# Learning loop with one gradient product per weight matrix, an early sum for weights 20, a new order of the loop's instructions, and expert tables made in two parts

## The chip, the cores and the metric

The kernel runs on one core of a Trainium2 chip. A core has TensorE (PE in the rows; its weight loads are PEld), VectorE (DVE), ScalarE (ACT), GpSimd (POOL) and SyncE (SP), each with a queue of its own that is worked off in order, and 16 DMA engines. The metric is the device time of one execution in microseconds (us), as the median over several runs. Everything is float32 unless a row says bf16.

## The reference

The input x is (4, 32, 32, 128). Three layers with residual sums follow each other: a memory that learns while it reads (the part that takes most of the time), a banded additive attention, and a top-2 mixture of 8 experts.

```python
def step(carry, x_t):                     # 32 steps, one after the other
    params, mom = carry                   # per batch b: w1_0, w2_0, w1_1, w2_1
    k = _l2norm(x_t @ Wk); v = x_t @ Wv   # 32 tokens of 128 per batch and step
    lr, forget, eta = ...                 # one number per batch and step
    g = grad_fn(params, k, v)             # of mean((mlp(params, k) - v) ** 2)
    new_mom = eta * mom - lr * g
    new_params = params * (1.0 - forget) + new_mom
...                                       # _mlp: h = h + gelu(h @ w1) @ w2, two layers
xn = (xt - mu) * rsqrt(var + LN_EPS)      # experts: 4096 tokens
probs = softmax(xt @ Wr + br); top_p, top_idx = top_k(probs, 2)
h = gelu(xe @ W1 + b1); y = h @ W2 + b2   # the two chosen of 8 experts, weighted and summed
```

## The kernel before, in words

The program is a row of blocks written out by hand: `prepare` (norms and projections), `learn` (the 32 steps), `read_out`, the attention, `experts`. In each block every engine has its own list of instructions, and semaphores alone tie the lists together. The order in a list is the order in the code. No scheduler moves anything.

**The learning loop (`learn`).** All four batches are worked on at once: a tile of 128 partitions holds 4 batches of 32 tokens. The four weight matrices are called 10 and 20 (first layer, up and down) and 11 and 21 (second layer). For each there are `W` (weights, 128 x 4 x 256, in the rows `s_w`), `M` (momentum, `s_w_mem`) and `KW` (weights times 1 - forget, `s_xsh`). The loop is rotated: one turn runs `backward(t)` and then `forward(t)`, which finishes step t and starts step t+1. Thirty-one turns follow each other, and `last` closes the block. Along a turn runs one chain, in which TensorE, ScalarE and VectorE take turns. Its VectorE instructions have names by which the turn can be cut in pieces:

- `l_h` (h1, the output of layer 1), then `l_g<-lp_b` on ScalarE (gelu of layer 2, called gelu1 below),
- `l_dp` (the error, dp), after it `l_dd`, `l_v` and `l_gp` (the slope of gelu in three instructions: `weighted`, `bent`, `slope`),
- `l_da<-l_gp,lp_a` (da1), `l_dh` (dh1), `l_da<-l_gp,lp_b` (da0), and so to the next `l_h`.

Between two of these lie a transpose on TensorE (`turn`), a copy out of PSUM on ScalarE (`feature`) and a product on TensorE (`up` or `down`, four batches side by side in strips of 32).

Beside the chain lies the upkeep of the weights. TensorE makes the gradient of a matrix in four PSUM banks `lp_g`, one per batch (`grad_1`, `grad_2`). VectorE then makes the new momentum of each batch (`momentum`, 16 instructions a turn). ScalarE or GpSimd makes KW (`keep_of`), and GpSimd (`add`, for 21, 11 and 10) or VectorE (`update`, for 20) makes W = KW + M. All four gradients go through the same banks, so a gradient waits until the momentum of the one before is done. Before the change a turn has six gradient groups: 20 and 11 are split into two pairs of batches each (`D11A, D11B, D20A, D20B`), 21 and 10 are whole (`D21, D10`). (The number names the momentum that the group feeds.) TensorE also transposes W of 21, 11 and 20 (`turn_w`, two halves each), and ScalarE copies them out (`wt`).

**The expert block (`experts`).** The 4096 tokens are routed in four groups (`routed(g)`, g = 0 to 3). GpSimd scatters every group's rows to their expert's region in DRAM (`f_xg`, 16 scatters a group). When all groups are routed, VectorE works out tables for 39 jobs of 256 rows: which expert owns a job (`owner_i`, `mine`) and at which row it starts (`start_i`). Jobs 0 to 16 (`NA` = 17) read only rows of the first three groups. SP loads a job's rows (`f_xt`), TensorE turns them (`turn(j)`) and multiplies, and 39 jobs follow each other at an even pace. SP starts with

```python
sp.wait_ge(owner_ready, 4)
sp.wait_ge(sent, 16 * 2 * GT * (GR - 1))      # scatters of groups 0 to 2
```

and TensorE, before its first job, makes the bias table from `mine` and runs 20 matmuls whose result is not used (`unused`).

Of the kernel before, what the change touches and what calls it, by code (L numbers as in the profile page):

```python
# [305 lines left out]
def learn(nc, st, sb):  # L306

    sem = lambda name: st.enter_context(nc.semaphore(name))
    with ExitStack() as ctx:
# [20 lines left out]
        ps_g = [bank(f"g{b}") for b in range(B)]  # L330
# [14 lines left out]
        G21, G11, G20, G10 = range(4)  # L345
        D21, D11A, D11B, D20A, D20B, D10 = range(1, 7)
# [32 lines left out]
        with nc.Block() as block:  # L379
# [10 lines left out]
            def _(pool):  # L390
# [21 lines left out]
                def forward(p, grads=True):  # L412
                    t = p + 1
                    if grads:
                        for k in ("21", "20", "10"):
                            pool.wait_ge(kept[k], p * 2 + 2)
                        pool.wait_ge(kept["11"], p * 2 + 2)
                    nc.gpsimd.tensor_copy(keep_lr[:, :], step_of(t, "coef")[:, 4:9]).then_inc(lr_in, 1)  # L418
                    pool.wait_ge(lr_in, t + 1)
                    nc.gpsimd.tensor_tensor(keep[:, :], keep_lr[:, 0:B], none[:, :], ALU.subtract).then_inc(keep_in, 1)  # L420
                    if grads:
                        add(p, "21", G21, 1)
                    if grads:
                        pool.wait_ge(grad_done, p * 6 + D10)
                    nc.gpsimd.tensor_copy(kc[:, :], step_of(t, "ktok")).then_inc(kc_ready, 1)
                    if grads:
                        add(p, "11", G11, 1)
                    keep_of(t, "11", 0)
                    if grads:
                        add(p, "10", G10, 0)  # L430
                    nc.gpsimd.tensor_copy(kx[:, :], step_of(t + 1, "kf")).then_inc(kx_ready, 1)
                    if grads:
                        pool.wait_ge(mom_ready, mom(p, G10, 1))
                    nc.gpsimd.tensor_copy(eta[:, :], step_of(t, "coef")[:, 0:4]).then_inc(eta_in, 1)
# [4 lines left out]
                    scaled(kk, keep).then_inc(kk_ready, 1)
                    keep_of(t, "11", 1)  # L440
                    if grads:
                        add(p, "10", G10, 1)

                def backward(t):
                    add(t, "21", G21, 0)
                    pool.wait_ge(mm_done, t * 7 + A0)
# [1544 lines left out]
```

## Time and profile before

| | before |
|---|---|
| three runs | 956.37, 959.83, 960.83 us, median 959.83 us |
| the profiled execution | 957.53 us, its span 955.7 us |
| busy share of the span | PE 85%, DVE 76%, ACT 65%, POOL 64% |
| one turn of the loop | 15.24 us, 31 turns |
| granted clock in the loop | 1.00 of 2.4 GHz |

The span is the time from the first to the last instruction of the profiled execution. A turn's length is the distance of two starts of the same instruction in neighbouring turns. The shares are averages over blocks with different limits, so what the change is worth is read within the loop and within the start of the expert jobs.

### The profile page before, as it was taken

Reading aid. Unit: us, or ns where it says so; the run is one execution under the profiler, and the core shown is the slowest. Engines: PE = TensorE matmul, PEld = TensorE weight load, DVE = VectorE, ACT = ScalarE, POOL = GpSimd, SP = SyncE. Lnnn points to the kernel's source line nnn. Section 1 sums busy time; section 2 is a strip of 40 time slices with the busy share of each in tenths; the row PEclk is TensorE's granted clock in tenths of the full one; section 3 lists DMA queues with packets and bytes.
Section 4 is the critical chain, followed back from the end, with each engine's and each line's share of the span. In section 5 each row is a group of like instructions: output and inputs, shape, how many; then the busy total and the mean of one; then the engine's idle time right before and its main releaser. Section 6 shows DMA issues by size and latency. Waiting matters only on the chain. (4 is left out here: it accounts for less than half of the span.)

```text
span 955.7 us, 25199 instructions
## 1 busy us (share of the span) xinstructions
PE 809.4 (85%) x8049; PEld 506.4 (53%) x8049; DVE 726.0 (76%) x1861; ACT 618.9 (65%) x1384; POOL 608.6 (64%) x758
## 2 busy tenths in 40 slices
PE   2788999999999999999999989965678777999950
PEld 2455555555555555555555544431246544999940
DVE  3586888888888888888888871578798875777747
ACT  4577777778777787877777753228823523888830
POOL 1127888878788887878788739940004777666650
PEclk8899999999999999999999999987998978999985
DMA  7006999996000000000000005005000113233327
GB/s 239 1 2 140 159 208 158 81 6 2 0 0 0 0 0 0 0 0 0 0 0 0 0 5 157 18 11 185 1 4 29 52 51 90 82 93 93 92 68 239
DMA packets 105406, 54.10 MB, mean 57 GB/s; under 512 B 42624, under 2 KB 96664, under 8 KB 105360
## 3 DMA queue, kind: packets, MB, share of 16 engines
q1 hardware_dynamic: 98976, 43.34, 28.9%
q0 software_dynamic: 4544, 9.38, 3.0%
q10 hardware_dynamic: 1840, 0.79, 0.3%
q8 instruction: 26, 0.43, 0.2%
q14 instruction: 20, 0.16, 0.1%
HBM read 21.49 MB, written 29.44 MB: 53 GB/s over the span
## 5 line engine op out<-in xcount | busy, mean ns | idle before, releaser
L398 POOL TENSOR_TENSOR s_w<-s_xsh,s_w_mem 128x512 f32<-128x512 f32 x186 | 252.0, 1355 | 9.0 <-DVE s_w_mem L570 3.5
L570 DVE SCALAR_TENSOR_TENSOR s_w_mem<-s_w_mem,s_eta,lp_g 128x256 f32<-128x256 f32 x496 | 218.0, 476 | 23.9 <-PE lp_g L733 18.6
L495 ACT ACTIVATE s_xsh<-s_w,l_keep_lr 128x256 f32<-128x256 f32 x384 | 173.9, 507 | 17.5 <-POOL l_keep_lr L418 17.5
L1489 POOL DMA_INDIRECT f_yg<-f_yr,f_xmeta x78 | 78.3, 1004 | 38.4 <-DVE f_yr L1857 25.6
L1484 POOL DMA_INDIRECT f_xg<-f_xrow,f_place x64 | 64.0, 1000 | 49.3 <-DVE f_place L1750 30.4
L403 POOL TENSOR_TENSOR s_xsh<-s_w,l_keep 128x512 f32<-128x512 f32 x64 | 72.0, 1125 | 0.0
L1464 ACT ACTIVATE f_hh<-fp_v,f_bcol 128x256 f32<-128x256 f32 x156 | 61.4, 476 | 14.4 <-DVE f_hs_lo L1848 8.5
L489 ACT COPY l_wt<-lp_b 128x512 f32<-128x512 f32 x96 | 56.5, 588 | 15.0 <-PE lp_b L719 15.0
L719 PE MATMUL lp_b<-s_cst,s_w 128*128 128x128 f32 x384 | 61.7, 284 | 0.0
L1594 PE MATMUL fp_v<-f_xf,s_w_hi 128*128 128x256 bf16 x312 | 54.4, 276 | 3.3 <-DVE f_xmeta L1837 2.7
L707 PE MATMUL lp_h<-s_w,l_gf 128*32 128x128 f32 x1024 | 41.4, 278 | 18.3 <-ACT l_gf L482 18.3
L719 PEld LDWEIGHTS lp_b<-s_cst,s_w 128*128 128x128 f32 x384 | 43.0, 141 | 23.2 <-DVE l_gp L602 13.2
L1848 DVE TENSOR_TENSOR f_hs_lo<-f_hh,f_hs_hi 128x512 bf16<-128x512 f32 x52 | 33.6, 688 | 21.4 <-ACT f_hs_hi L1470 21.4
L579 DVE TENSOR_TENSOR s_w<-s_xsh,s_w_mem 128x512 f32<-128x512 f32 x62 | 48.0, 775 | 1.1
L733 PE MATMUL lp_g<-l_dh,l_g 32*128 32x128 f32 x496 | 44.2, 296 | 0.0
L1177 DVE TENSOR_TENSOR t_h<-s_qp,s_kp 128x1056 f32<-128x1056 f32 x32 | 37.6, 1255 | 8.5 <-ACT s_kp L1200 8.3
L707 PEld LDWEIGHTS lp_h<-s_w,l_gf 128*32 128x32 f32 x1024 | 25.0, 109 | 35.4 <-issue 25.1
L726 PE MATMUL lp_g<-l_da,l_h 32*128 32x256 f32 x248 | 43.4, 426 | 0.0
L1594 PE MATMUL fp_v<-f_xf,s_w_lo 128*128 128x256 bf16 x156 | 43.1, 276 | 0.0
L489 ACT COPY l_wt<-lp_a 128x512 f32<-128x512 f32 x64 | 37.7, 589 | 6.7 <-PE lp_a L719 6.7
L719 PE MATMUL lp_a<-s_cst,s_w 128*128 128x128 f32 x256 | 42.0, 286 | 0.0
L733 PEld LDWEIGHTS lp_g<-l_dh,l_g 32*128 32x128 f32 x496 | 32.4, 185 | 16.5 <-DVE s_w_mem L570 12.8
(360 smaller groups left out, 2040.7 us busy)
## 6 DMA issues: line engine op xcount, KB each, us to landing
f_xg<-s_pad SPq DMA_DIRECT2D x1, 17280.0 KB, 108.2
f_xt<-f_xg SPq DMA_DIRECT2D x39, 130.0 KB
r_w<-in_L_ffn_W_dram SPq DMA_DIRECT2D x16, 256.0 KB, 3.2
s_w<-f_yg SPq DMA_DIRECT2D x16, 256.0 KB, 3.8
xs<-in_x_dram SPq DMA_DIRECT2D x4, 512.0 KB, 7.0
t_w<-in_L_ffn_W_dram SPq DMA_DIRECT2D x8, 256.0 KB
out_dram<-s_x SPq DMA_DIRECT2D x8, 256.0 KB, 3.1
s_xsh<-s_xl SPq DMA_DIRECT2D x4, 448.0 KB, 3.5
```

What stands on the lines that cost most here:

```text
L398: nc.gpsimd.tensor_tensor(W[k][:, half(h), :], KW[k][:, half(h), :], M[k][:, half(h), :], ALU.add).then_inc(w_ready[k], 1)
L403: nc.gpsimd.tensor_tensor(KW[k][:, half(h), :], W[k][:, half(h), :], keep[:, half(h)].rearrange("p (b a) -> p b a", a=1).to_broadcast([128 ...
L489: nc.scalar.copy(flat(WT[k][:, half(h), :]), wt_bank(k, h)).then_inc(wt_ready, 1)
L495: m = nc.scalar.mul(KW[k][:, b, :], W[k][:, b, :], keep_lr[:, b:b + 1])
L570: i = nc.vector.scalar_tensor_tensor(out=M[k][:, b, :], in0=M[k][:, b, :], scalar=eta[:, b:b + 1], in1=ps_g[b][:, 0:256], op0=ALU.mult, op ...
L707: i = nc.tensor.matmul(p[rows(b), 0:128], x[:, 128 * h + 32 * b:128 * h + 32 * b + 32], w[:, b, 128 * h:128 * h + 128], start=h == 0, stop ...
L719: i = nc.tensor.transpose(wt_bank(k, h)[:, 128 * j:128 * j + 128], W[k][:, 2 * h + j // 2, 128 * (j % 2):128 * (j % 2) + 128], ident)
L733: i = nc.tensor.matmul(ps_g[b][:, 128 * h:128 * h + 128], x[rows(b), 128 * h:128 * h + 128], y[rows(b), :], start=True, stop=True)
L1464: nc.scalar.activation(hh[j % 2][:, h, :], ps_h[j % 2][:, SL * h:SL * h + SL], ACT.Gelu, bias=bcol[:, h, j:j + 1]).then_inc(h_ready, 1)
L1484: nc.gpsimd.indirect_dma_start(sb["xg"][:, :], bass.IndirectOffsetOnAxis(ap=place[:, g, k, i:i + 1], axis=0), row[k][:, tile_of(g, i), :], ...
L1489: nc.gpsimd.indirect_dma_start(sb["yg"][:, :], bass.IndirectOffsetOnAxis(ap=xmeta[:, j, a, 0:1].bitcast(mybir.dt.int32), axis=0), yr[j % R ...
L1594: m = nc.tensor.matmul(p, chosen(w1s[b], e, h), xf[j % 2][:, c, :], start=r == 0, stop=r == 2)
```

## The change

Five things change in the loop, one in the expert block.

1. Each gradient is made for four batches in one group (`D21, D11, D20, D10`): two groups a turn less on TensorE.
2. Weights 20: instead of `momentum` and then W = KW + M in two halves, VectorE first makes P = eta * M + KW for each batch (`decayed_20`, four new instructions, before the gradient is there), then W = P + gradient for all four batches in one instruction of 1024 elements that reads PSUM (`update_20`). The momentum of 20 is still made, after it.
3. The momenta are made in another order of batches, each with a semaphore step of its own, and at other places of VectorE's list.
4. On TensorE the gradient of 21 stands ahead of the transpose of dp, the gradient of 10 behind the transpose of h1, and `turn_w("20", 1)` behind the product for gelu1. ScalarE copies that one out after gelu1 (`wt(t, X20B, ...)` moved from `forward` to `backward`) and makes the KW pieces in another order.
5. GpSimd copies `kx` at the head of its `forward`, makes `ke` in `backward`, and makes the adds of 11 in a row.
6. The tables of jobs 0 to 16 are worked out between the third and the fourth group's routing (`first_tables`). The rest follows after the fourth. SP waits for the first part only, and for the second at job 17.

```diff
-        ps_g = [bank(f"g{b}") for b in range(B)]
+        ps_all = bank("g", B)
+        ps_g = [ps_all[:, 512 * b:512 * b + 512] for b in range(B)]
...
-        D21, D11A, D11B, D20A, D20B, D10 = range(1, 7)
+        D21, D11, D20, D10 = range(1, 5)
+        KEEPS = {"21": (0, 2, 3, 1), "20": (0, 1, 2, 3), "10": (2, 0, 1, 3), "11": (0, 1, 2, 3)}
...
+                def decayed_20(t, b):
+
+                    dve.wait_ge(eta_in, t + 1)
+                    dve.wait_ge(kept["20"], kept_of(t, "20", (b,)))
+                    dve.wait_ge(mom_ready, mom(t - 1, "20", (b,)))
+                    nc.vector.scalar_tensor_tensor(out=P[:, b, :], in0=M["20"][:, b, :], scalar=eta[:, b:b + 1],
+                                                   in1=KW["20"][:, b, :], op0=ALU.mult, op1=ALU.add).then_inc(decayed_ready, 1)
+
+                def update_20(t):
+
+                    dve.wait_ge(decayed_ready, 4 * t + 4)
+                    dve.wait_ge(grad_done, t * 4 + D20)
+                    nc.vector.tensor_tensor(W["20"][:, :, :], P[:, :, :],
+                                            ps_all[:, :].rearrange("p (b n) -> p b n", b=B)[:, :, 0:256], ALU.add).then_inc(w_ready["20"], 4)
...
-                    momentum(t, "21", D21, (0,))
+                    momentum(t, "21", D21, 2, 3, 0)
                     slope_times(t, 1, ps_a, DG1)
-                    momentum(t, "21", D21, (1,))
-                    momentum(t, "21", D21, (2, 3))
-                    momentum(t, "11", D11A, (0, 1))
+                    momentum(t, "21", D21, 1)
+                    decayed_20(t, 0)
+                    decayed_20(t, 2)
+                    momentum(t, "11", D11, 0)
                     dve.wait_ge(mm_done, t * 7 + DH1)
...
-                sp.wait_ge(owner_ready, 4)
+                sp.wait_ge(owner_ready, 3)
                 sp.wait_ge(sent, 16 * 2 * GT * (GR - 1))
                 for j in range(NJ):
                     if j == NA:
+                        sp.wait_ge(owner_ready, 6)
                         sp.wait_ge(sent_last, 16 * 2 * GT)
...
+                def first_tables():
+                    filled(carry_a[:, :], tiles_a)
...
+                    beyond(0, NA, ends_a[:, 1:E])
+                    owners(0, NA)
...
+                    gaps(0, NA, gap_a)
+                    dve.wait_ge(owner_ready, 2)
+                    link(nc.vector.tensor_reduce(owner[:, 0:NA], past[:, 0:NA, :], AX.X, ALU.add))
+                    nc.vector.tensor_tensor(start_i[:, 0:NA], owner[:, 0:NA], job[:, 0:NA], ALU.add).then_inc(owner_ready, 1)
+
                 def routed(g):
                     bias_piece(2 * g)
+                    if g == GR - 1:
+                        first_tables()
                     dve.wait_ge(lg_done, 2 * g + 2)
```

**Where VectorE's list changes first: from the slope to da1.** Before, in `backward` (`s_w_mem` is a momentum, `l_da` da1; REGISTER_ALU and ISA rows prepare waits):

```order
L602 SCALAR_TENSOR_TENSOR l_gp<-l_v,lp_b 128x256
L567 REGISTER_ALU
L570 SCALAR_TENSOR_TENSOR s_w_mem<-s_w_mem,s_eta,lp_g 128x256
L607 REGISTER_ALU
L608 SCALAR_TENSOR_TENSOR l_da<-l_gp,lp_a 128x256
L570 SCALAR_TENSOR_TENSOR s_w_mem<-s_w_mem,s_eta,lp_g 128x256 x5
```

The same place now (`l_p` is the new early sum for weights 20):

```order
L626 SCALAR_TENSOR_TENSOR l_gp<-l_v,lp_b 128x256
L583 ISA
L586 REGISTER_ALU
L587 SCALAR_TENSOR_TENSOR s_w_mem<-s_w_mem,s_eta,lp_g 128x256 x2
L586 REGISTER_ALU
L587 SCALAR_TENSOR_TENSOR s_w_mem<-s_w_mem,s_eta,lp_g 128x256
L631 REGISTER_ALU
L632 SCALAR_TENSOR_TENSOR l_da<-l_gp,lp_a 128x256
L587 SCALAR_TENSOR_TENSOR s_w_mem<-s_w_mem,s_eta,lp_g 128x256
L594 ISA
L595 SCALAR_TENSOR_TENSOR l_p<-s_w_mem,s_eta,s_xsh 128x256
```

Three momenta stand ahead of da1 instead of one. Behind it come one momentum, two early sums and one more momentum instead of five momenta.

**The second place on VectorE: from da0 to h1.** Before (the two `s_w` rows are the two halves of `update`):

```order
L608 SCALAR_TENSOR_TENSOR l_da<-l_gp,lp_b 128x256
L578 ISA
L579 TENSOR_TENSOR s_w<-s_xsh,s_w_mem 128x512
L567 REGISTER_ALU
L570 SCALAR_TENSOR_TENSOR s_w_mem<-s_w_mem,s_eta,lp_g 128x256 x2
L578 REGISTER_ALU
L579 TENSOR_TENSOR s_w<-s_xsh,s_w_mem 128x512
L583 ISA
L584 SCALAR_TENSOR_TENSOR l_u<-l_q,lp_a 128x256
L590 SCALAR_TENSOR_TENSOR l_dd<-l_q,l_g 128x256
```

And now:

```order
L632 SCALAR_TENSOR_TENSOR l_da<-l_gp,lp_b 128x256
L594 REGISTER_ALU
L595 SCALAR_TENSOR_TENSOR l_p<-s_w_mem,s_eta,s_xsh 128x256
L587 SCALAR_TENSOR_TENSOR s_w_mem<-s_w_mem,s_eta,lp_g 128x256
L602 TENSOR_TENSOR s_w<-l_p,lp_g 128x1024
L587 SCALAR_TENSOR_TENSOR s_w_mem<-s_w_mem,s_eta,lp_g 128x256 x2
L637 ISA
L638 ISA
L638 TENSOR_TENSOR l_h<-lp_h,s_ktok 128x128
L587 SCALAR_TENSOR_TENSOR s_w_mem<-s_w_mem,s_eta,lp_g 128x256
```

The two updates became one with 1024 elements, and `l_u` and `l_dd` of the next step moved behind `l_h`.

**The place in the expert block, VectorE ahead of the fourth group's router.** Now (`f_tilesa`, `f_endsa`, `f_past`, `f_owner`: tables of the first 17 jobs; `f_lg` is the first instruction of the fourth group's routing):

```order
L1763 TENSOR_TENSOR f_tilesa<-f_endsa 128x8
L1747 TENSOR_TENSOR f_past<-s_job,f_endsa 128x119
L1751 TENSOR_REDUCE f_owner<-f_past 128x17
L1752 CAST f_owneri<-f_owner 128x17
L1753 TENSOR_SCALAR f_mine<-f_owner,s_cst 128x17
L1766 TENSOR_SCALAR f_gapa<-f_tilesa 128x7
L1756 TENSOR_TENSOR f_past<-f_past,f_gapa 128x119
L1769 TENSOR_REDUCE f_owner<-f_past 128x17
L1770 TENSOR_TENSOR f_starti<-f_owner,s_job 128x17
L1779 TENSOR_TENSOR f_lg<-fp_y,f_s 128x64
```

Before, all of it stood behind the fourth group, and `f_owner` and `f_past` were made for 39 jobs at once. Fourteen instructions moved ahead, and sixteen are left behind the fourth group where 26 stood.

## Rows read from the trace of the kernel before

**Rows 1.** The page: its first line, and the costliest group of copies on ScalarE (count | busy us, mean ns)

```profile
span 955.7 us, 25199 instructions
...
L489 ACT COPY l_wt<-lp_b 128x512 f32<-128x512 f32 x96 | 56.5, 588 | 15.0 <-PE lp_b L719 15.0
```

**Rows 2.** Busy time per engine in one turn (us, instructions, granted clock)

```profile
302.42:317.66 15.24, 14.58 (x175) 8.53 (x171) 12.86 (x33) 11.79 (x30) 12.51 (x17) 1.00 0.00 0
```

**Rows 3.** Instructions in order of time, VectorE, one turn (start us, duration us)

```profile
302.42 0.42 DVE L608 SCALAR_TENSOR_TENSOR l_da<-l_gp,lp_b 128x256 f32<-128x256 f32 x1
...
302.75 0.69 DVE L579 TENSOR_TENSOR s_w<-s_xsh,s_w_mem 128x512 f32<-128x512 f32 x1
...
304.25 0.87 DVE L579 TENSOR_TENSOR s_w<-s_xsh,s_w_mem 128x512 f32<-128x512 f32 x1
...
306.17 0.29 DVE L620 TENSOR_TENSOR l_h<-lp_h,s_ktok 128x128 f32<-128x128 f32 x1 [0.38 <-PE lp_h L707]
...
310.43 0.35 DVE L637 SCALAR_TENSOR_TENSOR l_dp<-lp_h,l_keep_lr,l_hv 128x128 f32<-128x128 f32 x1 [0.72 <-PE lp_h L707]
...
310.70 0.57 DVE L590 SCALAR_TENSOR_TENSOR l_dd<-l_q,l_g 128x256 f32<-128x256 f32 x1
...
312.57 0.42 DVE L608 SCALAR_TENSOR_TENSOR l_da<-l_gp,lp_a 128x256 f32<-128x256 f32 x1
...
312.90 2.21 DVE L570 SCALAR_TENSOR_TENSOR s_w_mem<-s_w_mem,s_eta,lp_g 128x256 f32<-128x256 f32 x5
...
315.02 0.28 DVE L648 TENSOR_TENSOR l_dh<-lp_h,l_dp 128x128 f32<-128x128 f32 x1
...
317.66 0.42 DVE L608 SCALAR_TENSOR_TENSOR l_da<-l_gp,lp_b 128x256 f32<-128x256 f32 x1
```

**Rows 4.** The same turn, TensorE and ScalarE

```profile
303.16 0.70 PE L745 MATMUL lp_a<-l_da,l_sk 128*128 128x256 f32 x2
...
308.21 0.38 ACT L468 ACTIVATE l_g<-lp_b 128x256 f32<-128x256 f32 x1
...
308.49 0.38 ACT L471 ACTIVATE l_q<-lp_b 128x256 f32<-128x256 f32 x1
...
311.10 0.73 PE L733 MATMUL lp_g<-l_dp,l_g 32*128 32x128 f32 x16
...
315.85 0.33 PE L713 MATMUL lp_t<-s_cst,l_dh 128*128 128x128 f32 x1
...
316.11 0.71 PE L733 MATMUL lp_g<-l_dh,l_g 32*128 32x128 f32 x8
```

**Rows 5.** The same turn, GpSimd

```profile
302.39 0.19 POOL L418 COPY l_keep_lr<-s_coef 128x5 f32 x1 [1.15 <-ACT s_xsh L495]
...
302.81 1.76 POOL L398 TENSOR_TENSOR s_w<-s_xsh,s_w_mem 128x512 f32<-128x512 f32 x1
...
305.90 1.28 POOL L398 TENSOR_TENSOR s_w<-s_xsh,s_w_mem 128x512 f32<-128x512 f32 x1
...
307.14 1.04 POOL L403 TENSOR_TENSOR s_xsh<-s_w,l_keep 128x512 f32<-128x512 f32 x1
```

**Rows 6.** Instructions in order of time, VectorE, the loop's last step

```profile
556.76 1.28 DVE L658 SCALAR_TENSOR_TENSOR s_w_mem<-s_w_mem,s_eta,s_xsh 128x256 f32<-128x256 f32 x2
```

**Rows 7.** Instructions in order of time, start of the expert jobs

```profile
779.80 0.23 DVE L1719 TENSOR_TENSOR f_lg<-fp_y,f_s 128x64 f32<-128x64 f32 x1 [3.05 <-PE fp_y L1532]
...
787.84 0.29 DVE L1794 TENSOR_TENSOR f_over<-f_carrya,s_lim 128x128 f32<-128x128 f32 x1
...
792.34 5.09 PE L1118 MATMUL fp_y<-s_w_hi 128*128 128x384 bf16 x20
...
795.48 18.55 SPq L1394 DMA_DIRECT2D f_xt<-f_xg  x8
...
799.30 0.40 PE L1565 MATMUL fp_x<-f_identb,f_xt 128*128 128x128 bf16 x4 [0.91 <-DMA f_xt<-f_xg]
```

**Rows 8.** Waits of SP's queue (waits for what: us in total, times, longest)

```profile
SPq L1393 <- DVE f_bcol L1829: 3.1, 1, 3.1
```

More of the change, by code:

```diff
@@ L360, in step_of, with mom, kept_of, weights_of @@
             return sb[k][:, bass.ds(t, 1), :].rearrange("p a n -> p (a n)")
-        def mom(t, n, h):
-            return t * 8 + 8 + 2 * n + h + 1
+        def mom(t, k, batches=range(B)):
+            return t * 16 + 16 + max(MOMENTA.index((k, b)) for b in batches) + 1
+        def kept_of(t, k, batches):
+            return t * 4 + max(KEEPS[k].index(b) for b in batches) + 1
+        def weights_of(t, k, h):
+            return t * 4 + 2 * HALVES[k].index(h) + 2
+        def of_half(h):
+            return (2 * h, 2 * h + 1)
         def wt_bank(k, h):
@@ L420, in forward @@
-                    nc.gpsimd.tensor_tensor(keep[:, :], keep_lr[:, 0:B], none[:, :], ALU.subtract).then_inc(keep_in, 1)
                     if grads:
[L422 to L427, printed above, removed]
+                        add(p, "11", 0)
@@ L428, in forward @@
                     keep_of(t, "11", 0)
                     if grads:
[L430 to L434, printed above, removed]
+                        add(p, "11", 1)
+                        pool.wait_ge(grad_done, p * 4 + D10)
@@ L435, in forward @@
+                    nc.gpsimd.tensor_copy(kc[:, :], step_of(t, "ktok")).then_inc(kc_ready, 1)
+                    keep_of(t, "11", 1)
                     pool.wait_ge(mm_done, t * 7 + A0)
                     pool.wait_ge(kx_ready, t + 1)
+                    pool.wait_ge(keep_in, t + 1)
+                    scaled(kk, keep).then_inc(kk_ready, 1)
+                    if grads:
+                        add(p, "10", 0)
+                        pool.wait_ge(mom_ready, mom(p, "10"))
+                    nc.gpsimd.tensor_copy(eta[:, :], step_of(t, "coef")[:, 0:4]).then_inc(eta_in, 1)
@@ L437, in forward, with backward @@
+                    if grads:
+                        add(p, "10", 1)
+                def backward(t):
+                    add(t, "21", 1)
+                    keep_for(t + 1)
                     pool.wait_ge(eta_in, t + 1)
                     scaled(ke, eta).then_inc(ke_ready, 1)
[L439 to L446, printed above, removed]
+                    add(t, "21", 0)
@@ L763, in forward @@
                     turn(h1, 128)
-                    pe.wait_ge(chain, t * 6 + K_HV)
-                    turn_w("20", 1)
-                    pe.wait_ge(w_ready["11"], t * 2 + 2)
+                    if grads:
+                        pe.wait_ge(mom_ready, mom(p, "20"))
+                        pe.wait_ge(kc_ready, p + 1)
+                        grad_1(kc, da[0], range(B))
+                    pe.wait_ge(w_ready["11"], t * 4 + 4)
                     pe.wait_ge(wt_ready, t * 6 + X21B)
```

245 lines of the change are left out of this document (121 added, 124 removed).

## The prediction

> **What bounds the kernel now.** I read four views in this order. The page gives the span, 955.7 us [rows 1]. The profiled execution took 957.53 us, 1.8 us more, and it lies 2.3 us under the median of the three runs, 959.83 us. Sums are made against 957.53 and then raised by 2.3. The busy times of one turn show a turn of 15.24 us in which PE is busy for 14.58, DVE for 12.86, ACT for 11.79 and POOL for 12.51, at a granted clock of 1.00 [rows 2]. No engine is full, so the turn is bounded by a chain that runs through three of them. In the instructions in order of time I cut this chain at the starts of VectorE's instructions [rows 3] and of gelu1 on ScalarE [rows 4]:
>
> - da0 (302.42) to h1 (306.17): 3.75
> - h1 to gelu1 (308.21): 2.04
> - gelu1 to dp (310.43): 2.22
> - dp to da1 (312.57): 2.14
> - da1 to dh1 (315.02): 2.45
> - dh1 to the next da0 (317.66): 2.64
>
> The sum is 15.24. Thirty-one turns are 472 us, half the span. The expert jobs start when two things are there: loaded rows, for which the second transpose at 799.30 waits [rows 7], and a TensorE that has finished its 20 unused matmuls. SP's first load leaves at 795.48 [rows 7]. The waits of SP's queue show that it waited 3.1 us for VectorE's tables after the scatters of the first three groups had landed [rows 8].
>
> **The loop, piece by piece.**
>
> TensorE. A gradient for two batches takes 0.71 us and one for four takes 0.73 [rows 4]. The strips run side by side, so two groups fewer save 1.4 us of TensorE a turn. That is worth something only where such a group stood in the chain.
>
> VectorE. A momentum in a row of five takes (2.21 - 0.47) / 4 = 0.435 us [rows 3]. Two updates go (0.69 + 0.87 [rows 3]). Four early sums come: 0.44 each if they are like a momentum, up to 0.64 when GpSimd is at work (1.28 for two [rows 6]). The 1024-element sum is not in the trace. From 0.42 for 256 elements and 0.69 for 512 [rows 3] one element costs 1.05 ns, so I estimate 1.22 us. Its bounds are 1.22, and twice 0.87 if it should be held up as the updates are. VectorE then needs 12.86 - 1.56 + 1.76 + 1.22 = 14.28 us a turn at least. So VectorE alone allows no turn under 14.3, and it is busy for 94% of a turn of 15.2. Its order now decides.
>
> - dp to da1: two more momenta stand in it, 2.14 + 0.87 = 3.01. Of this up to 0.15 may go, since `l_dd` took 0.57 where others of its size take 0.42 [rows 3]. I take 2.90. The gradient that now stands ahead of dp's transpose costs TensorE 0.7 here, but the product for da1 is ready at about 2.6 and hides under VectorE's 2.9. Without these momenta it would cost 0.5.
> - da1 to dh1: VectorE has five momenta between them today, which is all of the 2.45. Now it has two momenta and two early sums, 0.33 + 0.87 + 0.88 = 2.08, with held sums 2.5. TensorE's side becomes the longer: 0.86 until the last momentum of 21 is made, 0.65 for the whole gradient, 0.8 for the product and its way to VectorE, 2.31. I take 2.33.
> - dh1 to da0: the transpose of dh1 starts 0.83 after dh1 today (315.85 [rows 4]), behind half a gradient and the product of `kk`. With the gradient whole and ahead it starts when dh1 is done, at 0.35. So TensorE's side needs 1.9. VectorE has three momenta and one early sum to do, 0.2 + 1.31 + 0.44 = 1.95. I take 1.92 for 2.64. This is the gain of the change.
> - da0 to h1: the product of `sk` starts 0.74 after da0 (303.16 [rows 4]) where 0.42 and 0.05 would do, since the second half of a gradient is in front. It goes, so 3.48 to 3.54; I take 3.50. W of 20 comes after an early sum, a momentum and the long sum, 0.33 + 0.44 + 0.44 + 1.22 = 2.43 after da0, and must be there 0.8 ahead of h1, at 2.7. This holds with 0.2 to spare. Held like the updates, the long sum would come at 2.9 and cost 0.2.
> - h1 to gelu1: the gradient of 10 now stands ahead of the product for gelu1 and waits for a momentum made behind h1: 0.74 + 0.65 + 0.70 = 2.09. The product also waits for W of 11 on GpSimd. There, after ScalarE's last KW piece (as at 302.39 [rows 5], 2.6 after dh1), stand two copies (0.5), an add (1.28), a KW piece (1.1) and an add (1.28) [rows 5], 6.8 after dh1 against 1.92 + 3.50 + 1.39 = 6.8 for the gradient. So W of 11 is 0.05 to 0.25 late. I take 2.19 for 2.04.
> - gelu1 to dp: the copy of transposed weights 20 (0.59 [rows 1]) now stands between the square and the copy of gf1. With starts 0.28 apart (308.21, 308.49 [rows 4]) it begins at 0.56 and gf1 at 1.05, where transpose and latencies alone give 0.9. I take 2.37 for 2.22.
>
> The sum is 3.50 + 2.19 + 2.37 + 2.90 + 2.33 + 1.92 = 15.21 us. What the whole gradients give back behind dh1 is spent on VectorE ahead of da1. Thirty-one turns change by -0.9 us. With every piece at its low end I get 15.0, with every piece at its high end 15.55.
>
> `last` is reordered too (two early sums move behind dh1). I take nothing; bounds are 0 and minus one pair of such sums, 1.0 us.
>
> **The tables.** VectorE stands idle for 3.05 us ahead of the fourth group's first instruction at 779.80 [rows 7]. The first tables fill that. By their 14 instructions behind 787.84 [rows 7] I make them 3.4 us, so the fourth group starts 0.4 late, which its scatters do not feel since GpSimd is behind with the third group's. What is left behind it is 2.6 us shorter. SP loses its wait: the first load leaves 2.3 to 3.1 earlier. `mine` for the last jobs is ready 1.3 earlier, and TensorE's 20 matmuls (5.09 [rows 7]) end 1.3 earlier than 797.43, at 796.1. The second transpose then stands at 796.2 to 797.0 instead of 799.30. The jobs behind it keep their pace. I take -2.5 (bounds -2.3 and -2.8).
>
> Together -0.9 - 2.5 = -3.4 us: 954.1 for a run like the profiled one, and 956.4 on the scale of the median. It is 0.4% faster. Half a per cent (4.8 us) is about what a measurement of this kernel can tell from no change.
>
> **Rivals.**
>
> *A. The loop stays level* (a turn of 15.05 to 15.40), chance 0.48: -5.9 to +5.0 us in the loop, so 951.4 to 962.3. The forecast is in it.
>
> *B. The chain closes up*, 0.22. Early sums and `l_dd` are never held, W of 11 is in time, and latencies are shorter than I made them: a turn of 14.8 to 15.0, 31 x 0.34 = 10.5 less, and with the tables 946.8. For it speaks that the early sums stand where VectorE would otherwise wait for TensorE. Against it speaks that VectorE must be 96% full. It decides when the turn is under 15.18.
>
> *C. W of 11 late and sums held*, 0.16. GpSimd's five instructions ahead of the product for gelu1 leave nothing to spare. If the early sums hold up GpSimd's adds, as the update did at 302.81 (1.76 for 1.28 [rows 5]), W of 11 comes another 0.3 to 0.5 late: a turn of 15.6, 31 x 0.36 - 2.5 = 8.7 more, 968.5.
>
> *D. `l_dd` behind a GpSimd add*, 0.07. `l_dd` starts 0.27 after dp and sets da1. GpSimd's second add of 10 is free to start a few tenths later. If it comes first, `l_dd` waits it out: 1.28 less 0.14, some 1.1 us a turn, 31 x 1.1 - 2.5 = 31.6 more, 991. What speaks for it is the pair at 302.75 and 302.81: the update, first by 0.06, kept its 0.69, and the add took 1.76 [rows 3, 5]. It decides if dp comes 0.3 later against GpSimd than I made it. The Trainium skill (SBUF — State Buffer, section "SBUF: two separate sides") says that GpSimd and a VectorE instruction with two SBUF inputs share a port pair as an exclusive lock: whichever starts first keeps it for its whole instruction. The rows agree. By that rule the 1024-element sum, with one input in PSUM, is not held, and the four early sums can be.
>
> *E. The tables bring nothing*, 0.07: SP's load waits for scatters anyway, or TensorE's 20 matmuls end no earlier. Against it speaks the 3.1 us wait [rows 8]. Then 958.9.
>
> **How the numbers follow.** The boundaries are 955.0 and 964.6. Of A, 0.20 lies below the first and 0.28 between. B is all faster. C is slower with 0.12, D slower. E is same with 0.05 and faster with 0.02. So faster 0.44, same 0.37, slower 0.19. The likeliest case is A, at 956.4. Its own range is 951 to 962. The range to hold 8 in 10 leaves out D, the slow half of C and the tip of B: 947 to 967.
>
> **What the changed profile would show.** Right: turns of 15.1 to 15.3; 2.9 from dp to da1, with three momenta in a row ahead of da1; 1.9 from dh1 to da0; one 1.2 us sum of 1024 elements, ended ahead of the product for h1; VectorE busy for over 14 us a turn; SP's first load at about 793 less what the loop gives, without a wait for VectorE. Wrong: `l_dd` or early sums of 0.6 us and more, a wait of the product for gelu1 on GpSimd's `s_w` that is over 0.3, or a turn under 15.0, which would mean that I counted latencies twice.

## The result and the profile after

| | before | after |
|---|---|---|
| median of four runs each, same chip | 958.10 us | 987.80 us (986.13 to 991.97) |
| ratio to before, 95% interval | | 1.0319, 1.0285 to 1.0353 |
| span of the profiled execution | 955.7 us | 984.3 us, time 986.13 |
| turns of the loop | all 15.24 us | of 30, 19 of 15.8 us (the first 16.1), 11 of 17.2 to 17.3 us |

The change makes the kernel 3.2% slower. The forecast was 956.4 us. The page of the changed kernel gives busy time per engine, and then groups (busy us, mean ns, idle time before them):

```profile
span 984.3 us, 25548 instructions
...
PE 782.9 (80%) x8049; PEld 486.4 (49%) x8049; DVE 792.0 (80%) x1958; ACT 612.5 (62%) x1384; POOL 606.9 (62%) x757
...
L614 DVE SCALAR_TENSOR_TENSOR l_dd<-l_q,l_g 128x256 f32<-128x256 f32 x64 | 58.2, 909 | 0.0
...
L602 DVE TENSOR_TENSOR s_w<-l_p,lp_g 128x1024 f32<-128x1024 f32 x31 | 37.6, 1213 | 0.0
```

VectorE has 66 us more to do (726 before, 792 now). Of that `l_dd` (`weighted`) is a surprise: 64 instructions of 0.91 us on average, where [rows 3] has one at 0.57. (32 belong to each layer: those of layer 1 take 1.35 in nearly every step, those of layer 0 some 0.48.) The long sum of weights 20 takes 1.21 as estimated. The instructions of one turn in order of time (start, duration), VectorE and GpSimd, answer to [rows 3, 5]:

```profile
305.26 1.28 POOL L414 TENSOR_TENSOR s_w<-s_xsh,s_w_mem 128x512 f32<-128x512 f32 x1
...
306.47 0.20 POOL L456 COPY s_eta<-s_coef 128x4 f32 x1
306.57 0.35 DVE L659 SCALAR_TENSOR_TENSOR l_dp<-lp_h,l_keep_lr,l_hv 128x128 f32<-128x128 f32 x1 [0.34 <-PE lp_h L735]
306.62 1.29 POOL L414 TENSOR_TENSOR s_w<-s_xsh,s_w_mem 128x512 f32<-128x512 f32 x1
306.83 1.35 DVE L614 SCALAR_TENSOR_TENSOR l_dd<-l_q,l_g 128x256 f32<-128x256 f32 x1
...
308.30 0.42 DVE L621 SCALAR_TENSOR_TENSOR l_v<-lp_b,l_dd 128x256 f32<-128x256 f32 x1
...
309.10 1.26 DVE L587 SCALAR_TENSOR_TENSOR s_w_mem<-s_w_mem,s_eta,lp_g 128x256 f32<-128x256 f32 x3
...
310.27 0.41 DVE L632 SCALAR_TENSOR_TENSOR l_da<-l_gp,lp_a 128x256 f32<-128x256 f32 x1
```

GpSimd's second add of weights 10 starts at 306.62, `l_dd` at 306.83. `l_dd` ends at 308.18, behind the add, and everything on VectorE behind it, da1 too, is 0.93 us later than without the hold (experiment 3). So it is in 31 of the 32 steps. What happens on TensorE in the same turn:

```profile
308.51 0.64 PE L727 MATMUL lp_a<-l_wt,l_dpf 128*32 128x256 f32 x8 [0.46 <-ACT l_dpf L502]
...
309.23 0.66 PE L747 MATMUL lp_b<-s_cst,s_w 128*128 128x128 f32 x4
310.74 0.63 PE L741 MATMUL lp_t<-s_cst,l_da 128*128 128x128 f32 x2 [0.85 <-DVE l_da L632]
311.30 1.23 PE L754 MATMUL lp_g<-l_da,l_h 32*128 32x256 f32 x8
312.46 1.08 PE L735 MATMUL lp_h<-l_wt,l_daf 128*32 128x128 f32 x16
313.32 1.08 PE L727 MATMUL lp_a<-s_w,l_kk 128*32 128x256 f32 x8
```

and in the next turn, the last four groups again:

```profile
328.03 0.44 PE L741 MATMUL lp_t<-s_cst,l_da 128*128 128x128 f32 x2 [0.85 <-DVE l_da L632]
328.42 0.71 PE L754 MATMUL lp_g<-l_da,l_h 32*128 32x256 f32 x8
329.06 0.64 PE L735 MATMUL lp_h<-l_wt,l_daf 128*32 128x128 f32 x16
329.52 0.61 PE L727 MATMUL lp_a<-s_w,l_kk 128*32 128x256 f32 x8
```

TensorE stands idle for 0.46 us ahead of the product for da1, where it waits for ScalarE's copy of dp, and for 0.85 ahead of the transpose of da1, where it waits for the late da1. In the first turn its instructions behind that take 1.4 to 1.8 times as long. The windows (engine busy times, then granted clock) show why:

```profile
298.42:315.73 17.31, 14.82 (x175) 8.36 (x179) 15.15 (x36) 11.61 (x32) 12.12 (x16) 0.90 0.00 0
315.73:331.55 15.82, 13.35 (x175) 7.74 (x179) 14.96 (x35) 11.63 (x32) 12.06 (x16) 1.00 0.00 0
...
310.40:311.20 0.80, 0.46 (x2) 0.23 (x2) 0.80 (x3) 0.11 (x1) 0.80 (x1) 0.78 0.00 0
311.20:312.00 0.80, 0.80 (x9) 0.52 (x8) 0.80 (x2) 0.59 (x2) 0.80 (x3) 0.50 0.00 0
```

The granted clock falls to 0.50, that is from 2.4 to 1.2 GHz, at about 310.85 (0.78 in a window of 0.80 us), and by the windows behind these it is back at about 314.25. Such a turn is 1.44 us longer, and 11 of 30 are such. All cuts are at the starts named in the prediction:

| piece | before | forecast | after, short turn | after, long turn |
|---|---|---|---|---|
| da0 to h1 | 3.75 | 3.50 | 3.40 | 3.40 to 3.43 |
| h1 to dp | 4.26 | 4.56 | 4.70 | 4.70 |
| dp to da1 | 2.14 | 2.90 | 3.70 | 3.70 |
| da1 to dh1 | 2.45 | 2.33 | 2.22 | 3.17 to 3.36 |
| dh1 to da0 | 2.64 | 1.92 | 1.78 | 2.10 to 2.26 |
| turn | 15.24 | 15.21 | 15.80 | 17.20 to 17.31 |

The thirty turns in one window:

```profile
86.94:577.25 490.31, 415.88 (x5134) 238.44 (x5138) 450.75 (x1051) 348.37 (x902) 362.50 (x480) 0.96 0.37 33
```

From the first da0 (86.94, 89.06 before) to the 31st (577.25, 546.27 before) lie 490.3 us where 457.2 lay, 33.1 more. The first da0 is 2.1 earlier, and from the 31st to the end of the span it takes 2.4 less. That makes the 28.6 between the spans.

### The profile page after: what moved, and what is told of

Read it like the earlier page. It is cut to its first block and busy times, and to the rows that moved or that the text cites. A ratio compares the mean times of both kernels' runs of the same rounds, so it can differ in the third digit from the quotient of the medians.

```text
span 984.3 us, 25548 instructions
## 1 busy us (share of the span) xinstructions
PE 782.9 (80%) x8049; PEld 486.4 (49%) x8049; DVE 792.0 (80%) x1958; ACT 612.5 (62%) x1384; POOL 606.9 (62%) x757
## 5 line engine op out<-in xcount | busy, mean ns | idle before, releaser
L414 POOL TENSOR_TENSOR s_w<-s_xsh,s_w_mem 128x512 f32<-128x512 f32 x186 | 236.8, 1273 | 72.5 <-DVE s_w_mem L587 69.3
L1515 POOL DMA_INDIRECT f_yg<-f_yr,f_xmeta x78 | 90.1, 1155 | 23.8 <-issue 23.5
L1510 POOL DMA_INDIRECT f_xg<-f_xrow,f_place x64 | 63.7, 995 | 51.8 <-DVE f_place L1810 32.6
L419 POOL TENSOR_TENSOR s_xsh<-s_w,l_keep 128x512 f32<-128x512 f32 x64 | 66.5, 1040 | 4.4
L595 DVE SCALAR_TENSOR_TENSOR l_p<-s_w_mem,s_eta,s_xsh 128x256 f32<-128x256 f32 x124 | 62.5, 523 | 0.0
L614 DVE SCALAR_TENSOR_TENSOR l_dd<-l_q,l_g 128x256 f32<-128x256 f32 x64 | 58.2, 909 | 0.0
L502 ACT ACTIVATE l_dh1f<-lp_t 128x128 f32<-128x128 f32 x32 | 8.9, 277 | 53.1 <-PE lp_t L741 53.1
L439 POOL COPY l_kx<-s_kf 128x128 f32 (+1 forms) x32 | 9.3, 290 | 47.3 <-ACT s_xsh L513 47.3
L602 DVE TENSOR_TENSOR s_w<-l_p,lp_g 128x1024 f32<-128x1024 f32 x31 | 37.6, 1213 | 0.0
```

What stands on the lines that cost most here:

```text
L595: nc.vector.scalar_tensor_tensor(out=P[:, b, :], in0=M["20"][:, b, :], scalar=eta[:, b:b + 1], in1=KW["20"][:, b, :], op0=ALU.mult, op1=AL ...
L614: nc.vector.scalar_tensor_tensor(out=dd[l][:, :], in0=q[l][:, :], scalar=1.0 / 3.0, in1=g[l][:, :], op0=ALU.add, op1=ALU.mult).then_inc(dd ...
L1510: nc.gpsimd.indirect_dma_start(sb["xg"][:, :], bass.IndirectOffsetOnAxis(ap=place[:, g, k, i:i + 1], axis=0), row[k][:, tile_of(g, i), :], ...
L1515: nc.gpsimd.indirect_dma_start(sb["yg"][:, :], bass.IndirectOffsetOnAxis(ap=xmeta[:, j, a, 0:1].bitcast(mybir.dt.int32), axis=0), yr[j % R ...
```

## The experiments

Spans are those of the profiled executions. Ratios are to the kernel before on the same chip, with 95% intervals.

**1 and 2. Each half of the change alone.** The function `learn` of the changed kernel with `experts` of before, and the reverse. The line of `experts` on which SP's start hangs, for the first against the changed kernel, for the second against before:

```diff
-                sp.wait_ge(owner_ready, 3)
+                sp.wait_ge(owner_ready, 4)
...
-                sp.wait_ge(owner_ready, 4)
+                sp.wait_ge(owner_ready, 3)
```

> The changed learning loop with the expert tables of before. In the trace of the changed kernel the first product of the expert jobs stands 29.1 us later than before, and the end of the loop 30.95 later, so the tables seem to give back 1.9 there, and 0.5 more lies in the rest of the tail. If the two edits add up, this kernel takes 2 to 3 us more than the changed one: a span of 986.3 to 987.3 against 984.3. Rival: the tables gain nothing by themselves, and the 1.9 is something that the loop leaves behind (another clock or other transfers at the start of the experts); then the span is 984.3 within 0.5.

> The loop of before with the tables in two parts. If the edits add up, the span is 955.7 less 1.9 to 2.7, so 953.0 to 953.8, and a turn stays at 15.24. Rival: nothing gained, 955.7 within 0.5.

Measured: the loop alone 994.77 us, 1.0359 (1.0295 to 1.0422), span 995.1. The tables alone 955.34 us, 0.9972 (0.9942 to 1.0002), span 953.5, turns of 15.24. The loop carries the whole loss. Its span is 8 us above what I expected. I account for it by three differences to the changed kernel: 14 long turns instead of 11 (thirty turns take 4.4 more), a first da0 1.2 later, and 5.2 more behind the last da0 (396.9 against 391.7). The clock fell in each of its first four turns (busy times and granted clock of the four together):

```profile
88.17:157.43 69.26, 59.10 (x688) 33.37 (x692) 60.87 (x141) 46.45 (x121) 48.66 (x64) 0.90 1.20 184
```

The tables gain 0.3%, and the interval just reaches 1. What they do is clearer in the traces. SP's first load leaves 6.2 and 7.6 us behind the start of the 48th scatter (the last of the first three groups) with the old tables (789.27 to 795.48, 828.49 to 836.04), and 3.4 and 3.4 with the new ones (821.22 to 824.62, 790.24 to 793.59). So 2.8 to 4.2 us of waiting go, and what is left on SP are the scatters themselves. The products of the jobs start 2.9 nearer to that scatter in the changed kernel (8.1 against 11.0), but only 1.0 nearer with the tables alone (10.0). There the loaded rows are not the last to come: TensorE reaches the first transposes, at 798.98, without a wait, straight from its 20 unused matmuls. It was held up before them, in 36 other unused matmuls (from 787.84, 7.94 us), at a granted clock of 0.50 up to some 791.8.

**3. The add behind `l_dd`.** One wait on GpSimd, so that `l_dd` goes first.

```diff
                     if grads:
+                        pool.wait_ge(dd_ready, t * 2 + 2)
                         add(p, "10", 1)
```

> The changed kernel, but GpSimd's second add of weights 10 waits until VectorE's l_dd of layer 1 has ended. Theory 1 (the add, first by 0.21 us, holds l_dd for 0.9 us a turn): l_dd falls from 1.35 to about 0.42, the stretch from dp to da1 from 3.70 to 2.8 or 2.9, a fast turn from 15.8 to 14.9 or 15.0, 30 turns x 0.85 = 25 us. Theory 2 (TensorE's granted clock falls in 11 of 30 turns, at 1.44 us each, because TensorE stands idle ahead of the transposes of da1 while it waits for l_dd) adds that these turns go too, 15.8 us: a span of about 944. Rival to theory 2 (the clock falls for another reason): the 11 turns stay, span about 959. Rival to theory 1 (l_dd is long for another reason, or the product for da1 is as late): dp to da1 stays above 3.4, span over 975.

Measured: 944.71 us, 0.9861 (0.9802 to 0.9921), span 937.4. The same place in a turn:

```profile
303.21 0.35 DVE L660 SCALAR_TENSOR_TENSOR l_dp<-lp_h,l_keep_lr,l_hv 128x128 f32<-128x128 f32 x1 [0.34 <-PE lp_h L736]
303.47 0.42 DVE L615 SCALAR_TENSOR_TENSOR l_dd<-l_q,l_g 128x256 f32<-128x256 f32 x1
...
304.03 1.27 POOL L414 TENSOR_TENSOR s_w<-s_xsh,s_w_mem 128x512 f32<-128x512 f32 x1 [0.72 <-DVE l_dd L615]
...
305.97 0.41 DVE L633 SCALAR_TENSOR_TENSOR l_da<-l_gp,lp_a 128x256 f32<-128x256 f32 x1
```

The windows, of one turn and of thirty turns:

```profile
295.09:309.96 14.87, 13.25 (x175) 7.71 (x179) 14.02 (x36) 11.55 (x32) 12.13 (x16) 1.00 0.00 0
86.70:532.97 446.27, 397.60 (x5134) 231.58 (x5138) 420.99 (x1051) 346.53 (x902) 363.91 (x480) 1.00 0.41 37
```

`l_dd` is back at 0.42, dp to da1 is 2.77, every turn is 14.87 (the first 15.17) and the clock is 1.00 throughout. GpSimd waits 0.72 us a turn for it and no piece of the turn is longer for that. One wait turns 3.2% slower into 1.4% faster. (The profiled execution, 939.17 us, is the lowest of the four; its turns, not its span, are what I compare.) Both theories come out as expected, but this run doesn't part them. TensorE's place ahead of the product for da1, for comparison:

```profile
305.15 0.64 PE L728 MATMUL lp_a<-l_wt,l_dpf 128*32 128x256 f32 x8 [0.46 <-ACT l_dpf L503]
```

The 0.46 is here too, at full clock. What the held `l_dd` adds is the 0.85.

**4. Work for the idle TensorE.** It parts the clock from the held `l_dd`. `spare` issues 128x128 matmuls into columns of `lp_h` that nobody reads.

```diff
                     turn(dp, 128)
+                    spare(2)
...
                     turn_w("11", 1)
+                    spare(4)
                     pe.wait_ge(chain, t * 6 + K_DA1)
```

> The changed kernel with six matmuls of 128 columns whose results nobody reads, two behind the transpose of dp and four ahead of the wait for da1, where TensorE stands idle for 0.46 and 0.85 us. Theory 2 (that idle time lets the granted clock fall): the 11 turns of 17.25 become 15.8, the clock in the loop is 1.00, the span 984.3 - 15.8 = 968.5, and l_dd stays at 1.35. Rival (the clock falls for another reason): the span stays at 984 or grows by up to 0.1 x 30 = 3 us.

Measured: 975.93 us, 1.016 (1.0097 to 1.0224), span 973.5. The matmuls fill both gaps, and nothing on TensorE stretches:

```profile
304.45 0.61 PE L741 MATMUL lp_h<-s_cst 128*128 128x128 f32 x4
305.07 0.64 PE L727 MATMUL lp_a<-l_wt,l_dpf 128*32 128x256 f32 x8
305.80 0.66 PE L751 MATMUL lp_b<-s_cst,s_w 128*128 128x128 f32 x4
306.29 1.06 PE L741 MATMUL lp_h<-s_cst 128*128 128x128 f32 x8
307.30 0.44 PE L745 MATMUL lp_t<-s_cst,l_da 128*128 128x128 f32 x2
```

and in the window of thirty turns:

```profile
89.36:563.59 474.23, 438.52 (x5494) 273.12 (x5498) 448.94 (x1052) 348.95 (x902) 362.73 (x480) 1.00 0.38 34
```

All turns are 15.8, `l_dd` is still 1.35, the clock is 1.00. Thirty turns take 474.2 us instead of 490.3, 16.1 less where 15.8 was expected. The span is 5 us over the number given because this run began and ended later (first da0 at 89.36, and 394.5 us behind the last one against 391.7). So the fall of the clock is a second cost of the late da1, and it goes when TensorE's idle time is filled. How much idle time, or where, it takes is not shown by this run (see experiment 10). The Trainium skill (TensorE: Matmul & The Clock Gate, section "What's actually happening") says that a block which watches how busy TensorE has been sets its clock at one of two levels; the trace agrees (0.50 and 1.00, and nothing between them that lasts).

**5. `l_dd` with one input from PSUM.** Same place, same start behind the add.

```diff
-                    nc.vector.scalar_tensor_tensor(out=dd[l][:, :], in0=q[l][:, :], scalar=1.0 / 3.0, in1=g[l][:, :],
+                    if l:
+                        dve.wait_ge(tanh_ready[l], t + 1)
+                    nc.vector.scalar_tensor_tensor(out=dd[l][:, :], in0=q[l][:, :], scalar=1.0 / 3.0,
+                                                   in1=ps_b[:, 0:256] if l else g[l][:, :],
```

> The changed kernel with l_dd of layer 1 in its place, but with its second input taken from PSUM (the pre-activation) instead of from SBUF (the activation g), behind ScalarE's tanh; its output is therefore not the reference's. Theory 1, in the form that two inputs in SBUF make the difference: l_dd keeps 0.42 though GpSimd's add started 0.2 before it, dp to da1 is 2.77, a turn 14.9, all 30 turns at full clock, span 937 to 947 as with the add behind l_dd. Rival (any VectorE instruction that meets GpSimd's add waits): l_dd 1.35, turns of 15.8 and 17.25, span 973 to 995.

Measured: 943.61 us, 0.9843 (0.9804 to 0.9882), turns of 14.89.

```profile
307.69 1.27 POOL L414 TENSOR_TENSOR s_w<-s_xsh,s_w_mem 128x512 f32<-128x512 f32 x1
307.90 0.42 DVE L616 SCALAR_TENSOR_TENSOR l_dd<-l_q,lp_b 128x256 f32<-128x256 f32 x1
```

The add is first by 0.21 again and `l_dd` takes 0.42 beside it. It is the pair of inputs in SBUF that is held, not any instruction that meets the add. This is the rule that the prediction cited from the Trainium skill (SBUF — State Buffer, section "SBUF: two separate sides"), and here the runs bear it out on both sides.

**6 and 7. Who is first.** Small copies (n = 1 and n = 3) push the add back without a semaphore.

```diff
+                    for i in range(n):
+                        nc.gpsimd.tensor_copy(rest[:, 4 * i:4 * i + 4], step_of(t, "coef")[:, 0:4])
                     if grads:
                         add(p, "10", 1)
```

> The changed kernel with one small copy (0.15 us, nobody reads it) ahead of GpSimd's second add of weights 10. The add then starts 0.20 behind dp instead of 0.05, and l_dd at 0.26. First come, first served: l_dd is still held, 1.20 instead of 1.35, so the delay lengthens it less and the turn stays: l_dd ends with the add, 0.15 later than now, dp to da1 3.85, fast turns 15.95 or, as GpSimd's work behind it has slack, 15.9 to 16.0. Rival (it is the load on GpSimd that matters, not the order of starts): the same as with three copies.

> The same with three small copies (0.45 us). The add is due 0.50 behind dp, l_dd starts at 0.26 and is first: l_dd 0.42, dp to da1 2.77, turns of 14.9 at full clock, span 937 to 947, though the add waits some 0.2 and GpSimd has more to do than before. Rival as above: turns of 15.9 and more.

Measured: with one copy 982.34 us, 1.0215 (1.0157 to 1.0274), short turns of 15.91; with three 945.41 us, 0.9846 (0.9803 to 0.9889), turns of 14.95. First one copy, then three:

```profile
308.80 1.27 POOL L415 TENSOR_TENSOR s_w<-s_xsh,s_w_mem 128x512 f32<-128x512 f32 x1
308.89 1.47 DVE L617 SCALAR_TENSOR_TENSOR l_dd<-l_q,l_g 128x256 f32<-128x256 f32 x1
```

```profile
305.14 0.69 POOL L459 COPY l_rest<-s_coef 128x4 f32 x3
305.36 0.42 DVE L617 SCALAR_TENSOR_TENSOR l_dd<-l_q,l_g 128x256 f32<-128x256 f32 x1
305.79 1.27 POOL L415 TENSOR_TENSOR s_w<-s_xsh,s_w_mem 128x512 f32<-128x512 f32 x1
```

With the add 0.09 ahead `l_dd` takes 1.47 and ends behind the add again. With more work on GpSimd, but the add second, `l_dd` keeps its 0.42 and dp to da1 is 2.77. (The three copies take 0.69 where I said 0.45, so the add comes 0.69 behind dp, and W of 11 comes later too: the turn is 0.08 longer than in experiment 3.) The last step of the run with one copy shows the order at its sharpest: there `l_dd` starts at 580.79 and the add at 580.80, `l_dd` keeps its 0.42, and the add takes 1.54. My expectation said 1.20 for `l_dd` with one copy, which was a slip of sign: the later the add ends, the longer `l_dd` takes, 1.47. Its dp to da1 (3.85 said, 3.82 measured) and turn (15.95, 15.91) were right. I had not expected that only 4 of 30 turns are long here, against 11; that number moves with the run (14 in experiment 1).

**8. `l_dd` earlier.** VectorE's order instead of GpSimd's.

```diff
                         momentum(p, "10", D10, 1)
+                    weighted(t, 1)
                     slope_in(t, 1, ps_b)
...
-                    weighted(t, 1)
                     bent(t, 1, ps_b)
```

> The changed kernel with VectorE's l_dd of layer 1 moved ahead of the sum u (1.5 us ahead of dp) instead of behind dp; GpSimd is left alone. VectorE has 0.34 us of idle time ahead of dp to take it in, and dp to da1 loses VectorE's 0.33 to 0.46, down to what TensorE's product for da1 allows, about 2.62. If l_dd and GpSimd's kk and first add of 10 don't hold it up: turns of 14.7, some 5 us under the kernel in which the add waits. Rival (l_dd now meets the first add of 10, which starts some 0.2 behind it, or u and so tanh come late): l_dd over 0.9 and turns of 15.2 or more.

Measured: 941.17 us, 0.9808 (0.9755 to 0.9861), turns of 14.79. `l_dd` takes 0.42, dp to da1 is 2.64, which is TensorE's side as expected. GpSimd's first add of 10 now comes second and gives 0.06 (1.33 for 1.28). I had said 14.7: da1 to dh1 gave back 0.05. The same move is made in `last`.

**9. Both adds of weights 11 first**, on top of 8, to take away the 0.20 us that the product for gelu1 waits for GpSimd.

```diff
                         add(p, "11", 0)
-                    keep_of(t, "11", 0)
-                    if grads:
                         add(p, "11", 1)
+                    keep_of(t, "11", 0)
```

> The kernel with l_dd of layer 1 ahead of u, and on GpSimd both adds of weights 11 ahead of the first KW piece of 11 (an add, a piece, an add before). The product for gelu1 waited 0.19 us in every turn for the second add; that add now ends about 1.0 earlier. If this wait was the last of it, h1 to dp goes from 4.70 to 4.51, a turn from 14.79 to 14.60, 31 turns 5.9 us, span 934 against 939.9, time 935 against 941. Rival: l_dd of layer 0, which now starts while a KW piece runs instead of in the tail of an add, is held, or the KW pieces and kk come late for what needs them; then 14.8 or more.

Measured: 937.57 us, 0.9776 (0.9738 to 0.9813), turns of 14.70. VectorE around dp:

```profile
299.94 0.43 DVE L614 SCALAR_TENSOR_TENSOR l_dd<-l_q,l_g 128x256 f32<-128x256 f32 x1
...
300.30 0.41 DVE L608 SCALAR_TENSOR_TENSOR l_u<-l_q,lp_b 128x256 f32<-128x256 f32 x1
...
300.63 0.86 DVE L587 SCALAR_TENSOR_TENSOR s_w_mem<-s_w_mem,s_eta,lp_g 128x256 f32<-128x256 f32 x2
...
301.41 0.34 DVE L660 SCALAR_TENSOR_TENSOR l_dp<-lp_h,l_keep_lr,l_hv 128x128 f32<-128x128 f32 x1
```

The wait is gone and gelu1 comes 0.24 earlier behind h1 (2.09 for 2.33), but dp only 0.08, so the turn is 14.70 and not the 14.60 expected. Dp has no idle time in front of it: VectorE, which now makes `l_dd` ahead of dp, sets it. By its turns this is the fastest version, 2.2% under the kernel before. By the ratios alone it is not told apart from experiment 8: the intervals overlap.

**10. One momentum ahead of da1**, on top of 3.

```diff
-                    momentum(t, "21", D21, 2, 3, 0)
+                    momentum(t, "21", D21, 2)
                     slope_times(t, 1, ps_a, DG1)
-                    momentum(t, "21", D21, 1)
+                    momentum(t, "21", D21, 3, 0, 1)
```

> The kernel in which GpSimd's add waits for l_dd, with one momentum of 21 ahead of da1, as before the change, and three behind it (three and one in the changed kernel). My prediction charged the two momenta ahead of da1 at 0.87. By the trace VectorE sets da1 at 2.77, and TensorE's product with the gradient in front would allow about 2.6. So dp to da1 falls only to 2.6 to 2.65, and the whole gradient of 21, which needs all four momenta, comes 0.78 later: da1 to dh1 grows from 2.22 to 2.95 or 3.0. A turn of 15.45 to 15.55 against 14.86, span 18 to 20 us over 942, if TensorE keeps its clock. Rival (the momenta ahead of da1 cost their 0.87 and the gradient has slack): dp to da1 1.9 to 2.0, a turn of 14.3 to 14.6.

Measured: 972.71 us, 1.0142 (1.0098 to 1.0186), turns of 15.73. dp to da1 falls only to 2.64, as expected. da1 to dh1 grows to 3.22, more than the 3.0 expected. The list of waits has one more entry (us in total, times, longest):

```profile
PE lp_g L755 <- DVE s_w_mem L588: 22.8, 31, 0.7
```

and in one turn:

```profile
307.04 0.64 PE L728 MATMUL lp_a<-l_wt,l_dpf 128*32 128x256 f32 x8 [0.46 <-ACT l_dpf L503]
...
309.39 0.71 PE L755 MATMUL lp_g<-l_da,l_h 32*128 32x256 f32 x8 [0.74 <-DVE s_w_mem L588]
```

The whole gradient of 21 stands in front of the product for dh1 and waits 0.7 a turn for the fourth momentum. So the two momenta that the change moves ahead of da1 are no mere loss of 0.87: whole gradients need them there. The run shows something on the clock as well. TensorE stands idle for 0.46 and 0.74 in a turn, and by the windows it is busy for 13.3 of 15.7 us, as in a short turn of the changed kernel (13.35 of 15.82), yet the clock is 1.00 in all turns. So a wait of nearly this size need not cost the clock.

## Why the prediction was wrong

**The step that failed** is the term dp to da1, "I take 2.90". It took `l_dd` as free ("up to 0.15 may go"), and left the overlap with GpSimd's second add of weights 10 to rival D, "`l_dd` behind a GpSimd add", at 0.07. Measured are 1.35 for `l_dd` and 3.70 from dp to da1. Rival D's mechanism was right, and experiments 3, 5, 6 and 7 show it. Its placing and its chance were not. I wrote that it decides "if dp comes 0.3 later against GpSimd than I made it". dp to the add and dp to `l_dd` are 0.05 and 0.26 in the trace. The prediction has no sum for the start of this add, only that it is "free to start a few tenths later". It started 0.21 earlier than `l_dd`. The margin of 0.3 had no sum of its own behind it, so neither had the chance. The traces show that both sides part at two events that lie 0.04 apart: the second add of weights 11 on GpSimd ends at 303.26 (301.99 + 1.27), and the gradient of 10 on TensorE at 303.30 (302.59 + 0.71). The product for gelu1 waits for the add, GpSimd's copy `kc` for the gradient. Counted from the end of the add, GpSimd needs the copy (0.25 of waiting ahead of it), a KW piece, `kk`, an add and a copy until its next add at 306.62, 3.36 us. The chain needs the product, gelu1, a transpose, a copy and a product until dp, 3.31 us. In order of time:

```profile
301.99 1.27 POOL L414 TENSOR_TENSOR s_w<-s_xsh,s_w_mem 128x512 f32<-128x512 f32 x1
...
302.59 0.71 PE L754 MATMUL lp_g<-l_da,l_kc 32*128 32x256 f32 x8
303.50 0.64 PE L727 MATMUL lp_b<-s_w,l_h1f 128*32 128x256 f32 x8 [0.20 <-POOL s_w L414]
...
303.51 0.29 POOL L447 COPY l_kc<-s_ktok 128x128 f32 x1 [0.25 <-PE lp_g L754]
```

From there on each side is a row of fixed durations, and from the second step to the last but one the add starts 0.05 or 0.06 behind dp; at that distance it was a near certainty on one side.

**What I had no term for** is TensorE's clock. The prediction took 1.00 of the profile before as given. It did not stay so: a held `l_dd` cost 0.93 a turn directly and, with the 0.85 of idle time it made on TensorE, 1.44 more in 11 turns of 30. With that idle time filled (experiment 4) no turn was long.

**The sum, as measured.** Thirty turns: held `l_dd` 30 x 0.93 = 27.9, the clock 11 x 1.44 = 15.8, the rest of the loop's edit 30 x (14.87 - 15.24) = -11.1, together 32.6 of the 33.1 measured. That rival D's 991 lies near the result is luck in part: it held neither the clock nor that gain.

**The other pieces.** Without the hold and at full clock (experiment 3) the turn is 14.87 where I had 15.21, so rival B's size, with 0.22, and not A's, with 0.48, was the right one for the loop's own edit. Of B's reasons only the shorter latencies are borne out as they stand: `l_dd` is free only by the added wait, W of 11 was not in time, and one early sum a turn was held. Which of the five items of the loop brings how much is read from the pieces below; no run parts them.
- da0 to h1: 3.40 for 3.50. Right in kind; latencies were shorter than I made them.
- h1 to dp: 4.70 for 4.56. The product for gelu1 waits 0.20 for W of 11, as forecast (0.05 to 0.25). gelu1 came at 2.33, not 2.19, gelu1 to dp was 2.37 as said.
- dp to da1: 2.77 for 2.90 without the hold. VectorE sets it, as said. The 0.15 that `l_dd` took longer before is most of what goes from 3.01 (2.14 + 0.87); I had counted on 0.11.
- da1 to dh1 and dh1 to da0: 2.22 and 1.78 for 2.33 and 1.92. The gain of whole gradients is where I put it, and larger.
- VectorE is busy for 14.02 us a turn without the hold (experiment 3), under the 14.28 that I gave as the least.
- The early sums take 0.52 on average (124 of them), between the 0.44 and 0.64 that I gave as bounds. But 93 take 0.48 or less, and one in each turn takes 0.66: it starts at 310.99 beside GpSimd's add of 310.10 and ends at 311.65, 0.28 behind the add. So the sign "early sums of 0.6 us and more" came true as well, at some 0.19 us of VectorE's time a turn. The sum of 1024 elements takes 1.21 and is never held, though an add of GpSimd runs beside it in each turn.

**The tables.** I took -2.5 us. From the last da0 to the end it is 391.7 against 394.4 before, and SP's wait for VectorE is gone as forecast. But this stretch moves by several us from run to run (389.1 to 394.7 in the kernels with new tables), so the size is not settled better than the interval of experiment 2, -5.6 to +0.2 us. Rival E is not excluded as a part of it: with the tables early, the landing of scatters is what SP waits for, and with the tables alone TensorE's unused matmuls ended later behind the 48th scatter than before (8.9 against 8.2), where I had them 1.3 earlier.

**Left open**: why the number of long turns differs between runs with the same held `l_dd`, why the wait in experiment 10 leaves the clock alone, and what sets the 5 us by which the start and the tail of the program differ from run to run.

## What to carry to other kernels

When two engines share a resource for a whole instruction, don't ask how likely the overlap is: find the last events that the two sides wait for, add up each side from there, and compare. If the two starts are within a few tenths, order them on purpose, by a wait or by the order of one engine's work; here that was worth over 4% (1.0319 against 0.9861). And a stall ahead of TensorE can cost twice, once by its length and once by the clock (here 0.93 a turn and 1.44 in 11 of 30, in experiment 10 the length alone), so look at the granted clock turn by turn before a mean over the loop is believed.

## What the runs showed of the hardware that I had not expected

- Whoever comes second loses less than the whole overlap. `l_dd`, 0.09 or 0.21 us late behind GpSimd's add, ends 0.27 to 0.29 us after it (310.36 against 310.07, 308.18 against 307.91), though it takes 0.42 alone: it overlapped the add by 1.08 and lost 0.93. With GpSimd second it is alike: in [rows 3, 5] the update ends at 303.44, 0.63 behind the start of the add, and the add lost 0.48. My estimate from these rows is a loss of the overlap less some 0.15 on either engine.
- The clock fell in the same part of the turn each time, 0.4 to 1.2 us behind the start of da1, yet in only 4, 11 or 14 turns of 30. In between, turns with the same idle times kept 1.00.
